# A recurrence of 64 chunks on five engines: the state copy gets a signal of its own, and TensorE's loop takes four chunks a pass

## The reference

```python
def step(carry, inp):
    W1c, b1c = carry
    xq, xk, xv, et = inp
    Z1 = xk @ W1c + b1c
    grad = _ln_l2_bwd(Z1, xv - xk, g, bb)
    Attn1 = jnp.tril(xq @ xk.swapaxes(-1, -2))
    b1_bar = b1c - jnp.tril(et) @ grad
    Z1_bar = xq @ W1c - et * Attn1 @ grad + b1_bar
    last_eta = et[..., -1, :, None]
    W1n = W1c - (last_eta * xk).swapaxes(-1, -2) @ grad
    b1n = b1c - (last_eta * grad).sum(-2, keepdims=True)
    return ((W1n, b1n), xq + _ln(Z1_bar, g, bb, EPS_IN))
```

## Time and profile before

| what | value |
|---|---|
| median of three runs | 635.27 us (635.17 to 635.96) |
| the profiled execution: its own time | 634.28 us |
| its span in the trace | 632.2 us |
| the scan, first L942 to last L942 of the 64 chunks | 166.6 to 486.2 us |
| mean granted clock of TensorE | 0.726 of full speed; about 0.5 in the scan |

### The profile page before, as it was taken

How to read it: one execution, slowest core, us unless ns; L and a number is a source line. 1 busy time by engine, 2 the same in 40 slices (tenths; PEclk the granted TensorE clock), 3 DMA queues, 4 the chain that set the end, 5 groups by cost and what they waited for, 6 DMA issues and landing times. The chain is left out here.

```text
span 632.2 us, 29743 instructions
## 1 busy us (share of the span) xinstructions
PE 503.4 (80%) x12294; PEld 358.3 (57%) x12294; DVE 468.7 (74%) x1446; ACT 358.2 (57%) x1164; POOL 333.8 (53%) x590
## 2 busy tenths in 40 slices
PE   0389988888448888888888888887787579959996
PEld 0144433444337877777777777777676234427663
DVE  6366888888547888888888888888888347555662
ACT  0344444312436777777777788877676258635321
POOL 1258888878325555555556555555654267540112
PEclk9999999989655555555556655556555679989999
DMA  8201111112660000000000000000000800000113
GB/s 342 81 0 35 36 36 37 39 38 51 148 137 5 1 0 1 0 1 1 0 1 1 1 1 0 1 1 1 1 1 5 289 2 1 2 1 2 68 67 133
DMA packets 11233, 24.76 MB, mean 39 GB/s; under 512 B 3140, under 2 KB 3880, under 8 KB 10920
## 3 DMA queue, kind: packets, MB, share of 16 engines
q1 hardware_dynamic: 11176, 24.09, 12.6%
HBM read 11.50 MB, written 4.19 MB: 25 GB/s over the span
## 5 line engine op out<-in xcount | busy, mean ns | idle before, releaser
L821 PE MATMUL PS<-work 32*32 32x32 f32 x4064 | 83.1, 236 | 40.2 <-DVE work L983 31.9
L821 PEld LDWEIGHTS PS<-work 32*32 32x32 f32 x4064 | 79.1, 150 | 51.4 <-issue 48.6
L1056 POOL TENSOR_TENSOR work<-work,mask 128x256 f32<-128x256 f32 x64 | 46.8, 731 | 91.0 <-DVE work L983 72.2
L810 PE MATMUL PS<-work 64*32 64x64 f32 x2048 | 69.5, 309 | 19.9 <-ACT work L1143 16.5
L810 PEld LDWEIGHTS PS<-work 64*32 64x32 f32 x2048 | 55.5, 163 | 27.0 <-issue 25.5
L833 PE MATMUL PS<-work 32*64 32x32 f32 x2016 | 67.0, 288 | 1.0 <-issue 1.0
L833 PEld LDWEIGHTS PS<-work 32*64 32x64 f32 x2016 | 58.6, 212 | 5.1 <-issue 1.1
L510 PE MATMUL PS<-X,work 128*128 128x512 f32 x128 | 59.8, 612 | 0.1
L1040 POOL TENSOR_TENSOR work<-KP,cst 128x256 f32<-128x256 f32 x64 | 39.3, 614 | 22.7 <-DVE work L945 17.1
L629 POOL TENSOR_TENSOR work<-work 128x512 f32<-128x512 f32 x32 | 43.9, 1372 | 5.3 <-DVE work L572 4.7
L1177 ACT ACTIVATE work<-PS,small 128x128 f32<-128x128 f32 x64 | 23.5, 367 | 40.8 <-PE PS L810 40.8
(11 more groups left out here) (157 smaller groups left out, 1243.3 us busy)
## 6 DMA issues: line engine op xcount, KB each, us to landing
X<-in_x SPq DMA_DIRECT2D x4, 1024.0 KB, 8.1
TK<-KP SPq DMA_DIRECT2D x64, 64.0 KB, 1.9
X<-QP SPq DMA_DIRECT2D x8, 512.0 KB, 8.9
TK<-in_x SPq DMA_DIRECT2D x4, 1024.0 KB, 8.2
out<-TK SPq DMA_DIRECT2D x16, 256.0 KB, 2.4
work<-in_rope SPq DMA_DIRECT2D x2, 512.0 KB, 9.3
cst<-in_consts SPq DMA_DIRECT2D x1, 289.0 KB, 4.9
work<-in_wk SPq DMA_DIRECT2D x1, 256.0 KB, 11.4
```

The lines of the kernel that those rows point to most:

```text
L810: mm = nc.tensor.matmul(PS[HD * a:HD * a + HD, ZB[p], b * ZW:b * ZW + ZW], KT2[p][r:r + 64, k * B + b, :, :].rearrange("p e t -> p (e t)") ...
L821: mm = nc.tensor.matmul(PS[HD * a:HD * a + HD, bank, b * width:b * width + HD], AM[p][HD * a:HD * a + HD, b, part, :, :].rearrange("p e t ...
L1056: nc.gpsimd.tensor_tensor(AM[p].rearrange("p b s e t -> p (b s) e t"), S1[p].unsqueeze(2).broadcast_to([P, 2 * B, E, CS]), mask2.rearrange ...
```

## The change

The state copy on ACT waits for a new signal, `updw`, that the last matmul of L833 raises; the bias copy goes on waiting for `upd`. On TensorE two chunks at either end are unrolled instead of four, and the loop's body holds four chunks instead of two. `past` now answers for a loop whose least c is 2.

```diff
-            names = ("init wcopy bcopy kt2 ...
+            names = ("init updw wcopy bcopy kt2 ...
...
             def past(c, n):
-                return c >= n if isinstance(c, int) else n <= 4
+                return c >= n if isinstance(c, int) else n <= 2
 
             def run_chunks(eng, body):
-                for c in range(4):
+                for c in range(2):
                     body(c, c % 2)
-                with eng.Fori(2, NC // 2 - 2) as pair:
-                    c = pair * 2
-                    body(c, 0)
-                    body(c + 1, 1)
-                for c in range(NC - 4, NC):
+                with eng.Fori(0, NC // 4 - 1) as four:
+                    for k in range(4):
+                        body(four * 4 + (2 + k), k % 2)
+                for c in range(NC - 2, NC):
                     body(c, c % 2)
...
                     for b in range(B):
                         for a in range(4):
                             k, a2 = divmod(a, 2)
-                            nc.tensor.matmul(PS[2 * HD * a2:2 * HD * a2 + 2 * HD, WB + k, b * HD:b * HD + HD],
+                            mm = nc.tensor.matmul(
+                                PS[2 * HD * a2:2 * HD * a2 + 2 * HD, WB + k, b * HD:b * HD + HD],
...
+                    mm.then_inc(q["updw"], 1)
                     for a in range(4):
...
                     if past(c, 1):
+                        act.wait_ge(q["updw"], c + 0)
+                        state_w(1 - p).then_inc(q["wcopy"], 1)
                         act.wait_ge(q["upd"], c + 0)
-                        state_w(1 - p).then_inc(q["wcopy"], 1)
                         state_b(p)
```

More of the change, by code:

```diff
@@ L755, in build @@
         with nc.Block() as block:
-            names = ("init wcopy bcopy kt2 qt2 qr kr khx base qbase corr s1 am z p sq ss sz zc v sd r ts y yp m u u2 "
+            names = ("init updw wcopy bcopy kt2 qt2 qr kr khx base qbase corr s1 am z p sq ss sz zc v sd r ts y yp m u u2 "
                      "yl c w yc gl upd attn zq sqq ssq sdq rq zn zt ot").split()
@@ L832, in update @@
                             k, a2 = divmod(a, 2)
-                            nc.tensor.matmul(PS[2 * HD * a2:2 * HD * a2 + 2 * HD, WB + k, b * HD:b * HD + HD],
-                                             KHX[p][HD * a:HD * a + HD, b, :, :].rearrange("p e d -> p (e d)"),
-                                             GL[p][HD * a:HD * a + HD, b, :],
-                                             start=False, stop=True, skip_group_check=True)
+                            mm = nc.tensor.matmul(
+                                PS[2 * HD * a2:2 * HD * a2 + 2 * HD, WB + k, b * HD:b * HD + HD],
+                                KHX[p][HD * a:HD * a + HD, b, :, :].rearrange("p e d -> p (e d)"),
+                                GL[p][HD * a:HD * a + HD, b, :],
+                                start=False, stop=True, skip_group_check=True)
+                    mm.then_inc(q["updw"], 1)
                     for a in range(4):
```

## The result

The kernel after the change took 630.44 us (median of 4 runs, 629.99 to 633.09) against 635.29 for the kernel before: ratio 0.9937, 95% interval 0.9916 to 0.9958. A second comparison on another occasion gave 630.91 against 636.04, ratio 0.9922 (0.9908 to 0.9937). So it is faster by 4.9 and 5.1 us. The forecast was 2.7 less, 632.6, with a range from 631.0; the direction and the mechanism of the priced parts were right, the gain was 1.8 times the forecast, and the median lies 0.6 under the range.

What follows compares the result with a forecast made beforehand. DVE was taken as nearly the bound, waiting on a short trip through TensorE that is late at back edges. Gains of 1.2 + 0.6 + 0.9 = 2.7 us gave 632.6 us, range 631.0 to 634.8.

Steps and rivals of the forecast that it cites:

- The back edge: TensorE's loop: 13 of 27 taken edges go, each gaining 0.09 us, 1.2 us in all.
- The copy's signal: ACT's state copy L1143 starts 0.04 us earlier, counting only at the 14 edges left: 0.6 us.
- The end: Last chunks of the scan: with only 62 and 63 unrolled, TensorE's stops for code go, 0.9 us.
- The opening: First chunks, slowed by instruction fetch: nothing booked, with 0.5 us either way.
- The sum: Whole kernel: 1.2 for edges, 0.6 for the state copy, 0.9 for the end, 2.7 us gained.
- (a): TensorE's loop: four-chunk body does not stay on chip, 3.2 to 7.0 us a pass lost, 680 us; chance 0.08.
- (b): Edges, copy and end: edges already paid back, at most 1.0 us gained, 634.3 us; chance 0.14.
- (c): DVE's L945: early signal ends its meeting with GpSimd's L1048, chunks near 4.70, 3.1 us more, 629.5; chance 0.06.
- (d): ACT's state copy: its earlier signal gains nothing, the rest holds, 633.2 us; chance 0.72 together with the forecast.
- part 2: ACT's state copy released by the end of L833 instead of L839: 0.6 us, bounds zero and 1.7.
- The rule on fetching: TensorE's back edge: the skill's two-page window would force fetches; prediction trusted the trace and expected four chunks to stay.

Runs made afterwards that it cites:

- early queries on before: Kernel before, with only GpSimd's copy of the queries (L1048) moved ahead of the wait for the gradient: 635.42 us, ratio 1.0001.
- experiment 6: GpSimd's query copy L1048 moved ahead of the gradient wait: on after 625.46 and 626.00 us, on before 635.42, with copy's signal and loop in pairs 625.69.
- run 15: Not a run's label: part of "was run 15 times", the 15 passes of the four-chunk loop body in the kernel after, 630.44 us.

## Why the prediction was right, and where it was short

- *The back edge.* Right in kind and size. A removed edge turns 5.03 + 4.70 into 2 x 4.82; the traces of after show 4.82 wherever no edge and no late chunk is near. 13 x 0.09 = 1.2 stands.
- *The copy's signal.* The mechanism held to the hundredth (0.19 behind L1205, gain only at the edges), the size was short: 0.07 an edge and not 0.04, because the copy's two instructions also run 0.024 shorter. The prediction read the copy at 338.83 for its start alone; its row already had 0.42 in place of 0.45. At the 13 edges of the loop's stretch that is 0.9 in place of 0.5. It is a mis-sized term.
- *The end.* 0.9 forecast, 1.2 measured.
- *The opening.* I booked nothing, with 0.5 either way. That bound was too narrow. Two traces of the same kernel differ there by up to 1.8, and after shows 1.3 less on average, of which I can place nothing firmly: the copy alone gave nothing there, the loop alone 0.8 in one trace. The range did not even hold the 0.5 allowed here: with it, it would have begun at 630.5, still a hair above the median of 630.44.
- *The clock.* Left out. In the scan the granted clock is 0.50 for most of the time, with single stretches at 1.00. In the first trace of after three chunks between 8 and 60 ran TensorE's L820 at the full clock, 0.45 us in place of 0.65, and came about 0.2 sooner, in the second trace four, and two more in its opening; in the traces of before it were two and none. The matmuls of such a chunk and the granted clock in it (PEclk, the figure behind POOL's: 1.00 in the second stretch, 0.51 in the first):

```profile
308.90 0.45 PE L820 MATMUL PS<-work 32*32 32x32 f32 x32 [0.49 <-DVE work L984]
```

```profile
304.00:308.50 4.50, 4.17 (x168) 3.79 (x168) 3.89 (x16) 3.38 (x15) 2.74 (x7) 0.51 0.00 0
308.70:311.00 2.30, 1.69 (x104) 1.53 (x104) 2.24 (x10) 1.84 (x9) 1.96 (x4) 1.00 0.00 0
```

That is 2.5 chunks more on average, 0.5 of the 2.6 us of the loop. The last column of the table above goes with one part of the change: the seven traces with the copy's own signal and code that stays on chip have 3 to 6 such chunks, the five without the signal 0 to 2. The mean granted clock of all executions says the same, profiled or not:

| kernel | median (lowest to highest) | before, beside it |
|---|---|---|
| copy's signal only | 0.7295 (0.727 to 0.734) | 0.718 (0.714 to 0.723) |
| copy's signal only, again | 0.7265 (0.723 to 0.737) | 0.714 (0.712 to 0.720) |
| loop of four only | 0.7195 (0.717 to 0.726) | 0.718 (0.714 to 0.723) |
| ends only | 0.715 (0.713 to 0.717) | 0.716 (0.713 to 0.724) |
| early queries on before | 0.714 (0.712 to 0.718) | 0.714 (0.712 to 0.720) |
| after, again | 0.7315 (0.724 to 0.736) | 0.718 (0.714 to 0.723) |

With the signal as the only edit the ranges don't overlap, twice; with the loop, the ends or the queries as the only edit the clock stays where it was. So the full-clock chunks come with the signal, a share of the gain that nothing had forecast. How the signal brings them is open, and the four executions of after in the first comparison had only 0.717 to 0.725. A scan shorter by 3 us would by itself raise the mean by some 0.001 (an estimate from 632 us at 0.718).
- *The sum.* 1.2 for the edges, 0.9 for the copy and 0.5 for the clock in the loop, 1.2 for the end and 1.3 for the opening are 5.1, against 4.9 and 5.1 by the medians. What failed is the size of four terms: the copy (0.6 booked, 0.9 in the loop), the end (0.9 and 1.2), and the opening and the clock, both booked at nothing (1.3 and 0.5). The priced terms came out by their own mechanisms; 1.8 of the 5 us came from the two that were left at nothing.
- *The rivals.* (a) fell: no packet in the loop. Its price of 1.2 to 5.0 us an edge and 0.5 a chunk fits six chunks a pass, where the branch takes 3.4 and the whole came out 55 us slower than after. (b) fell: the 1.2 of the end and 0.9 of the copy both came. (c) named the right lever, L1048 over L945, and rightly said that this change doesn't pull it; experiment 6 pulled it, and four more microseconds came. (d), that part 2 does nothing, is refuted by its own runs.
- *The rule on fetching.* I took the trace over the Trainium skill's window of two pages, and the empty queue q8 in the profile after bears that out for a body of four chunks. The 28 passes that the prediction counts between 206 and 468 us are 27, since the first ended at 204.3; nothing hangs on it.

What stays open: for the copy's signal alone and for the versions with early queries the medians show 1 to 2 us more gain than the three stretches of their traces; the time outside the scan doesn't show it, since it varies by 3 us between executions. The parts do not add up either: by the medians of one group the signal alone gives 2.8 us and the loop alone 4.0, both together 5.1.

One thing can be settled from the traces. ACT's copy is shorter when it was not held by its signal. In before and the other kernels with the old signal nearly every copy starts 0.067 us after the end of L839 and takes 0.445 or 0.446 (306 of 325). In the seven traces with the own signal 432 of 448 start 0.19 behind the variance and take 0.42, whether L839 ended shortly before them, as at 301.51 in after (301.48), or ended after they began, as with early queries, by 0.10. So it isn't the company of L839's writes that makes the copy longer. Why a copy that has been held takes 0.024 more isn't shown.

## What to carry to other kernels

A signal that covers more work than its reader needs should be split, but its worth is the distance to the next thing that holds the reader (0.05 us here, not 0.4) and only at the places where the reader's chain is the late one; its larger worth can be what it opens, as the early queries did. A loop over code on TensorE should be no longer than what stays on chip; below that, two and four chunks a pass came out alike once two chunks and not four were unrolled at either end. Unrolled code of small matmuls cost more here than it saved: measure the branch's own row and the instruction queue, not the count of instructions. When a removed delay seems to gain 0.3 us a time, look whether the chunk behind it is short because of the delay. And compare the granted clock of all executions, not only of the profiled one: a term of 0.2 us a time can hide there.

## What the runs showed of the hardware

- TensorE's code came in packets of 16 KB every 3.9 us, in the loop of six and unrolled alike. A taken branch cost 0.21 us with its target on chip and 3.4 us without.
- A body of 1344 matmul and weight-load records was run 15 times, the last 14 without one such packet; a body of 2016 brought 65 packets in 252 us.
- Two ACT instructions that copy PSUM took 0.422 us when they followed ACT's own work, 0.446 when their signal had held them (0.067 us from the end of the last matmul to their start).
- In kernels whose copy had a signal of its own and whose code stayed on chip, 3 to 6 chunks of the scan ran at the full clock, 0 to 2 in the others; a group of 32 matmul records took 0.45 us there and 0.65 elsewhere.
- A GpSimd copy of 128 x 128 float32 that ran over a DVE product of two SBUF operands stretched that product from 0.29 to 0.41 us; over DVE's L971 and L975, where it went in experiment 6, it stretched neither (0.42 and 0.18 us with it, 0.42 and 0.17 for L970 and L974 of before). GpSimd's L1096, two additions of 128 x 512 elements (2.49 us), stretched L974 to 1.17 and L978 from 0.29 to 1.32.
- The same rows of registers, waits and matmuls from a back edge to the next L942 took 1.587 us in one kernel with a loop in pairs and 1.635 in another whose loop lies at a different place in the code.
